# A chain of two mixings and two grouped convolutions on four row tiles: the first mixing moved from the whole array onto 32-row tiles

## The reference

```
# layers 0 and 2 ("mixing"): a matrix of its own for each sequence
h     = gelu(gelu(cond @ W0 + b0) @ W1 + b1)
att   = softmax(h @ W2 + b2)                    # 8 weights
agg_w = einsum('bk,koi->boi', att, weight)      # 128 x 128 for each sequence
x     = x + einsum('boi,bih->boh', agg_w, x) + (att @ bias_k)[:, :, None]
# layers 1 and 3 ("conv"): 4 groups of 32 channels, 9 taps, padding 4
x     = x + conv1d(x, w, groups=4) + (cond @ c_w.T)[:, :, None] + bias[:, None]
```

## Time and profile before

| | |
|---|---|
| median of 3 runs | 3080.31 us (3079.63 to 3084.73) |
| the profiled execution's own time | 3082.17 us |
| its span | 3080.3 us, mean granted clock 0.986 |
| PE / PEld busy | 97% / 86% |
| DVE / ACT / POOL busy | 44% / 44% / 58% |
| matmuls of the two convolutions (L301) | 36864 |
| matmuls of the second mixing (L316) | 6144 |
| matmuls of the first mixing (L289) | 1536 |
| DMA | 468.6 MB, the queue takes 47.7% of 16 engines |

### The profile page before, as it was taken

The page is one execution under the profiler, slowest core; times in us unless marked ns, Lnnn a source line. Parts: engine busy times, 40 slices in busy tenths (PEclk is TensorE's granted clock), DMA queues, the critical chain, the costliest instruction groups (busy, mean ns, idle before and its releaser), DMA issues.

```text
span 3080.3 us, 110157 instructions
## 1 busy us (share of the span) xinstructions
PE 3002.8 (97%) x44644; PEld 2650.9 (86%) x44644; DVE 1353.9 (44%) x2142; ACT 1362.7 (44%) x2358; POOL 1798.5 (58%) x1796
## 2 busy tenths in 40 slices
PE   4899999999999999999999999999999999999996
PEld 3788888888888888888888888888888888888885
DVE  5444444444444444444444444444444444444441
ACT  4344444444444444444444444444444444444442
POOL 0556656656655655655655655655655655655652
PEclk6999999999999999999999999999999999999998
DMA  7344444444444444444444444444444444444443
GB/s 317 103 146 153 152 145 154 152 145 154 152 145 154 152 145 154 152 145 154 152 145 154 152 145 154 152 145 154 152 145 154 152 144 154 152 144 155 152 145 105
DMA packets 229383, 468.62 MB, mean 152 GB/s; under 512 B 47336, under 2 KB 129392, under 8 KB 195312
## 3 DMA queue, kind: packets, MB, share of 16 engines
q1 hardware_dynamic: 229360, 468.30, 47.7%
HBM read 182.89 MB, written 150.99 MB: 108 GB/s over the span
## 4 chain that ended last, share of the span: by engine, by line
PE 96%; DMA 1%; DVE 1%; ACT 1%; SPq 0%; issue 0%; POOL 0%; POOLq 0%; DVEq 0%; ACTq 0%
PE ps L301 72%; PE ps L289 12%; PE ps L316 12%; DMA mixed<-work 1%; DMA conv_raw<-conv_w 0%; DVE y L571 0%; SPq L221 0%; DVE work L542 0%; ACT work L395 0%; PE ps L272 0%; DVE y L526 0%; DMA work<-mix_b 0%; ACT xp L382 0%; POOL work L628 0%; PE ps L244 0%
## 5 line engine op out<-in xcount | busy, mean ns | idle before, releaser
L301 PE MATMUL ps<-y,conv_parts 32*128 32x512 f32 x36864 | 2282.6, 392 | 6.8 <-DVE y L571 6.7
L301 PEld LDWEIGHTS ps<-y,conv_parts 32*128 32x128 f32 x36864 | 2026.2, 183 | 224.9 <-DVE y L571 81.0
L571 DVE SCALAR_TENSOR_TENSOR y<-ps,bias,y 128x512 fp32r<-128x512 f32 x1536 | 1035.6, 745 | 1662.4 <-ACT y L421 1662.3
L421 ACT ACTIVATE y<-ps,bias 128x512 fp32r<-128x512 f32 x1536 | 916.1, 699 | 721.1 <-PE ps L301 691.6
L609 POOL COPY bias<-bias_table 128x4 f32 (+1 forms) x512 | 324.5, 634 | 837.7 <-DMA work<-work 715.5
L621 POOL TENSOR_TENSOR xp<-x_t,xp 128x512 fp32r<-128x512 f32 x512 | 775.2, 1552 | 0.0
L448 ACT ACTIVATE work<-ps,bias 128x512 f32<-128x512 f32 x512 | 309.9, 689 | 853.9 <-PE ps L301 853.9
L628 POOL COPY work<-work 128x512 f32<-128x512 f32 x512 | 512.2, 1123 | 23.1 <-DMA work<-work 23.1
L613 POOL TENSOR_TENSOR m_parts<-m_raw,m_parts 128x128 fp32r<-128x128 f32 (+1 forms) x256 | 225.4, 880 | 416.6 <-ACT m_parts L428 416.6
L316 PE MATMUL ps<-y,m_parts 32*128 32x512 f32 x6144 | 414.0, 392 | 1.6 <-DVE y L571 1.5
L289 PE MATMUL ps<-xp,m_parts 128*128 128x512 f32 x1536 | 393.0, 404 | 20.7 <-POOL xp L621 20.7
(11 more groups left out here) (38 smaller groups left out, 36.4 us busy)
## 6 DMA issues: line engine op xcount, KB each, us to landing
x_t<-x SPq DMA_DIRECT2D x128, 1024.0 KB, 4.8
work<-work SPq DMA_DIRECT2D x2048, 64.0 KB, 2.0
out<-work SPq DMA_DIRECT2D x128, 1024.0 KB, 4.1
m_raw<-mixed SPq DMA_DIRECT2D x640, 64.0 KB, 3.3
mixed<-work SPq DMA_DIRECT2D x8, 2048.0 KB, 7.8
work<-mix_w SPq DMA_DIRECT2D x2, 2048.0 KB, 12.6
conv_raw<-conv_w SPq DMA_DIRECT2D x2, 768.0 KB, 10.9
work<-small SPq DMA_DIRECT2D x1, 852.0 KB
```

Source lines behind the costliest of these rows:

```text
L301: last = nc.tensor.matmul(ps[:, 4 + g, :], conv_parts[layer][rows, w, s, :], src[rows, a, p_in, q:q + N], start=(s == 0 and n == 0), stop= ...
L421: nc.scalar.activation(dst, ps[:, k if layer % 2 == 0 else 4 + k, :], ACT.Identity, bias=bias[layer][:, k:k + 1]).then_inc(high_set[layer], 1)
L571: nc.vector.scalar_tensor_tensor(out=dst, in0=ps[:, k if layer % 2 == 0 else 4 + k, :], scalar=bias[layer][:, k:k + 1], in1=high.bitcast(f ...
```

## The change

The first mixing is written like the second: 4 groups of 32 input channels, accumulated on four row tiles, where tile t now makes a quarter of *time* (512 consecutive points) rather than a phase, from x loaded so that partition 32q + c holds channel c of each group g at quarter q. It needs its matrix four times over (one copy for each 32 partitions), loaded and split like the second one's. Its banks hold quarters of time with all phases mixed, so ACT and DVE read a bank by phase (`by_phase`, every fourth element) and write four runs of 128 into `y1` (`segment`). PE's tasks are generated by one loop over rounds and tiles; with `LAG = 0` the order of the rounds is that of before, and in each round the four tiles follow each other. `x_high` waits once for the whole first mixing of the sequence before; the second mixing waits for `low` of layer 1 group by group.

```diff
-        x_t = sb("x_t", [128, T])
-        xp = sb("xp", [128, 2, PH, N], f32r)
+        x_t = sb("x_t", [128, G, N])
+        xp = sb("xp", [128, 2, G, N], f32r)
...
-        m_raw = {0: sb("m_raw0", [128, C]), 2: sb("m_raw2", [128, G, C])}
-        m_parts = {0: sb("m_parts0", [128, 2, C], f32r), 2: sb("m_parts2", [128, 2, G, C], f32r)}
+        m_raw = {l: sb(f"m_raw{l}", [128, G, C]) for l in (0, 2)}
+        m_parts = {l: sb(f"m_parts{l}", [128, 2, G, C], f32r) for l in (0, 2)}
...
+        def by_phase(q):
+            return ps[:, q, :].rearrange("c (m p) -> c p m", p=PH)
+        def segment(part, q):
+            return y1[:, part, :, 1 + q * (N // PH):1 + (q + 1) * (N // PH)]
...
-            def load_matrix0(j):
-                sp.dma_start(m_raw[0][:], scratch[0][bass.ds(j, 1)].rearrange("s (i o) -> (s i) o", i=C)).then_inc(m_in[0], 16)
-            def load_matrix2(j):
-                for p in range(PH):
-                    sp.dma_start(m_raw[2][CG * p:CG * (p + 1)],
-                                 scratch[1][bass.ds(j, 1)].rearrange("s (g c o) -> (s c) g o", g=G, c=CG)).then_inc(m_in[2], 16)
+            def load_matrix(layer, j):
+                for q in range(G):
+                    sp.dma_start(m_raw[layer][CG * q:CG * (q + 1)],
+                                 scratch[layer // 2][bass.ds(j, 1)].rearrange("s (g c o) -> (s c) g o", g=G, c=CG)).then_inc(m_in[layer], 16)
             def load_x(j):
-                sp.dma_start(x_t[:], x[j]).then_inc(x_in, 16)
+                for q in range(G):
+                    sp.dma_start(x_t[CG * q:CG * (q + 1)],
+                                 x[j].rearrange("(g c) (q n) -> q c g n", g=G, q=G)[q]).then_inc(x_in, 16)
...
-            def mix0(j, first):
-                pe.wait_ge(m_set[0], j + 1)
-                for p in range(PH):
-                    pe.wait_ge(x_low_set, nth(j, p))
-                    if not first:
-                        pe.wait_ge(low_set[2], nth(j - 2, p))
-                    for n, (m, a) in enumerate(PASSES):
-                        last = nc.tensor.matmul(ps[:, p, :], m_parts[0][:, m, :], xp[:, a, p, :], start=(n == 0), stop=(n == 2))
-                    last.then_inc(mm[0], 1)
+            MIX, CONV = G * len(PASSES), SHIFTS * len(PASSES)
+            ROUNDS = 2 * (MIX + CONV)
+            LAG = 0
+            def mix(layer, j, t, k, src, wait_src, wait_bank):
+                rows = slice(CG * t, CG * (t + 1))
+                g, n = divmod(k, len(PASSES))
+                m, a = PASSES[n]
+                if t == 0 and k == 0:
+                    pe.wait_ge(m_set[layer], j + 1)
+                if t == 0 and n == 0:
+                    pe.wait_ge(wait_src, nth(j, g))
+                if k == 0:
+                    wait_bank(t)
+                ins = nc.tensor.matmul(ps[:, t, :], m_parts[layer][rows, m, g, :], src[rows, a, g, :],
+                                       start=(k == 0), stop=(k == MIX - 1))
+                if k == MIX - 1:
+                    ins.then_inc(mm[layer], 1)
...
+            def step(i, inner):
+                for r in range(ROUNDS):
+                    for t in range(G):
+                        own = r - LAG * t
+                        if own >= 0:
+                            tile_round(i, inner, t, own)
+                        elif inner or i >= 0:
+                            tile_round(i - 1, inner, t, own + ROUNDS)
...
-                    for p in range(PH):
-                        high(0, i, p, y1[:, HIGH, p, 1:N + 1], not inner and i == 0)
+                    for q in range(G):
+                        high(0, i, q, segment(HIGH, q), by_phase(q), not inner and i == 0)
...
-                    for p in range(PH):
-                        low(0, i, p, y1[:, LOW, p, 1:N + 1], y1[:, HIGH, p, 1:N + 1])
+                    for q in range(G):
+                        low(0, i, q, segment(LOW, q), by_phase(q), segment(HIGH, q))
...
-                dve.wait_ge(x_in, 16 * (j + 1))
-                xv = x_t[:].rearrange("c (n p) -> c p n", p=PH)
-                for p in range(PH):
-                    if not first:
-                        dve.wait_ge(mm[0], nth(j - 1, p))
-                    nc.vector.tensor_copy(xp[:, HIGH, p, :], xv[:, p, :]).then_inc(x_high_set, 1)
+                dve.wait_ge(x_in, 16 * G * (j + 1))
+                if not first:
+                    dve.wait_ge(mm[0], 4 * j)
+                for g in range(G):
+                    nc.vector.tensor_copy(xp[:, HIGH, g, :], x_t[:, g, :]).then_inc(x_high_set, 1)
```

More of the change, by code:

```diff
@@ new lines, in conv @@
+            def conv(layer, j, t, k, src, wait_src, wait_bank):
+                rows = slice(CG * t, CG * (t + 1))
+                s, n = divmod(k, len(PASSES))
+                q, p_in = divmod(s, PH)
+                w, a = PASSES[n]
+                if k == 0:
+                    if t == 0:
+                        pe.wait_ge(wait_src, nth(j, PH - 1))
+                    wait_bank(t)
+                ins = nc.tensor.matmul(ps[:, 4 + t, :], conv_parts[layer][rows, w, s, :], src[rows, a, p_in, q:q + N],
+                                       start=(k == 0), stop=(k == CONV - 1))
+                if k == CONV - 1:
+                    ins.then_inc(mm[layer], 1)
@@ L322, in step, with tile_round, free0 @@
+            def tile_round(i, inner, t, r):
                 now, last, before = has(i, inner, 0), has(i, inner, 1), has(i, inner, 2)
-                if now:
-                    mix0(i, not inner and i < 2)
+                def free0(q):
+                    if inner or i >= 2:
+                        pe.wait_ge(low_set[2], nth(i - 2, q))
                 def free3(g):
@@ L342, in free1 @@
                         pe.wait_ge(low_set[1], nth(i - 1, g))
[L344 to L351, removed]
+                if r < MIX:
+                    if now:
+                        mix(0, i, t, r, xp, x_low_set, free0)
+                elif r < MIX + CONV:
+                    if before:
+                        conv(3, i - 2, t, r - MIX, y3, low_set[2], free3)
+                elif r < 2 * MIX + CONV:
+                    if last:
+                        mix(2, i - 1, t, r - MIX - CONV, y2, low_set[1], free2)
+                elif now:
+                    conv(1, i, t, r - 2 * MIX - CONV, y1, low_set[0], free1)
+            def step(i, inner):
[6 more added lines that the diff above has]
+                            tile_round(i - 1, inner, t, own + ROUNDS)
             steps(step)
@@ L412, in _, with high @@
             act.wait_ge(agg_mm, 2 * Q * QB)
-            def high(layer, j, k, dst, first):
+            def high(layer, j, k, dst, src, first):
                 act.wait_ge(mm[layer], nth(j, k))
@@ L451, in step @@
                     for p in range(PH):
-                        high(2, i - 1, p, y3[:, HIGH, p, 1:N + 1], not inner and i == 1)
+                        high(2, i - 1, p, y3[:, HIGH, p, 1:N + 1], ps[:, p, :], not inner and i == 1)
                 if now:
@@ L586, in step @@
                     for g in range(G):
-                        low(1, i - 1, g, y2[:, LOW, g, :], y2[:, HIGH, g, :])
+                        low(1, i - 1, g, y2[:, LOW, g, :], ps[:, 4 + g, :], y2[:, HIGH, g, :])
                 if now:
-                    for p in range(PH):
-                        low(0, i, p, y1[:, LOW, p, 1:N + 1], y1[:, HIGH, p, 1:N + 1])
+                    for q in range(G):
+                        low(0, i, q, segment(LOW, q), by_phase(q), segment(HIGH, q))
                 if has(i, inner, -1):
@@ L594, in step @@
                     for p in range(PH):
-                        low(2, i - 1, p, y3[:, LOW, p, 1:N + 1], y3[:, HIGH, p, 1:N + 1])
+                        low(2, i - 1, p, y3[:, LOW, p, 1:N + 1], ps[:, p, :], y3[:, HIGH, p, 1:N + 1])
             steps(step)
@@ L616, in x_low @@
             def x_low(j):
-                xv = x_t[:].rearrange("c (n p) -> c p n", p=PH)
-                for p in range(PH):
-                    pool.wait_ge(x_high_set, nth(j, p))
-                    nc.gpsimd.tensor_tensor(xp[:, LOW, p, :], xv[:, p, :], xp[:, HIGH, p, :].bitcast(fp32),
+                for g in range(G):
+                    pool.wait_ge(x_high_set, nth(j, g))
+                    nc.gpsimd.tensor_tensor(xp[:, LOW, g, :], x_t[:, g, :], xp[:, HIGH, g, :].bitcast(fp32),
                                             ALU.subtract).then_inc(x_low_set, 1)
```

20 lines of the change are left out of this document (9 added, 11 removed).

## The result

| | before | after |
|---|---|---|
| median of 17 runs | 3082.36 us (3078.75 to 3084.73) | 3087.14 us (3084.31 to 3089.18) |
| ratio | | 1.0015, 95% interval 1.0008 to 1.0022 |
| the profiled execution's own time, its span | 3082.17, 3080.3 | 3089.18, 3087.4 |

The change makes the kernel 4.8 us slower, +0.15%, which is within the 0.2% called "no change" above though the interval excludes zero. The forecast was +4 us and +0.13%. The 27 executions of the kernel before in one of the comparisons fall in two groups, 12 of 3078.9 to 3080.9 us at a mean granted clock of 0.987 or 0.988 and 13 of 3083.4 to 3084.9 us at 0.985 or 0.986, so a median of 3, as the 3080.31 of the prediction was, can stand 2 us beside that of 17.

The account below looks back on a forecast made before the run. Bound: the 3.50 us chain of ACT's and DVE's reads, not PE's work. Profiled execution 3082.2 + 4 (fill) + 0 x 127 = 3086.2; for the median, 3080.3 + 4 = 3084.3 us, +0.13%; range 3076 to 3096.

Parts of the forecast that it names:

- What bounds: Loop step: one ACT read, then DVE's four, set the fourth tile's start at 3.50 us; mix0 lies beside them.
- The switches, 0.25 us a step: Around mix0 on PE: 0.16 + 0.09 us a step removed, turning into a longer wait; taken as 0.
- the switches are paid for after all: Rival, in the loop: restart sooner by 0.25 us a step, gain 127 x 0.25 = 32, 3052 us; chance 0.11.
- Layer 0's reads by phase: ACT's and DVE's strided bank reads after the first mixing: 745 ns as now, costing only above 2.07 us each.
- POOL's contiguous x_low: POOL's low part of x on contiguous slices: 1.29 us for 1.50, four in the fill giving -0.8 us.
- x in the loop: Loads of x in the loop: landing 1.3 to 2.5 us later, with cover, so 0.
- The fill, +4: First sequence, before the loop, uncovered: terms sum to +3.8 us, taken as +4 (2 to 6).
- The tail: Fill, from the end of `x_low` to conv(1): 4.5 us instead of 2.59, so +1.9.
- The rhythm: Loop steps alternating 23.08 and 23.19 us might settle differently: -4 if all short, +10 if all long.
- the second rival: At conv(1)'s last round every step falls on ACT's late notice, 0.08 us each: 3094 us; chance 0.13.

Follow-up runs that it names:

- two cut kernels: Kernel before and changed kernel, each with ACT's and DVE's layer 1 work on 128 of 512 columns: 3052.64 us and 2987.65 us.
- run 1: Kernel before with ACT's and DVE's layer 1 work on 128 of 512 columns: 3052.64 us, ratio 0.9904.
- PE was kept busy: Changed kernel with useless matmuls into an unused bank while PE waits in the fill: 3085.90 us, ratio 1.0014.
- LAG = 1: Changed kernel with each tile one round behind the one before it, instead of none: 2995.77 us, ratio 0.9720.

## Why the prediction was right, and where it was not

- **What bounds.** Right, and for the reason given: the 3.50 us from ACT's first read to the fourth bank, seen with mix0 and without it, stood at 3.50 in the changed kernel and in the kernels with less and with more PE work (up to 3.51 with more). Cutting it short freed 99.5 us in the changed kernel.
- **The switches, 0.25 us a step.** This term was mis-sized: 0.58, from the two cut kernels. The working had 0.16 for the mixing's length, where the cut kernels show 0.19, and 0.09 for its entry, where they show 0.30; it had nothing for the 0.09 behind it. It didn't matter for the sum, since a gain beside the chain is worth nothing whatever its size; for the rival "the switches are paid for after all" it would have meant 3011 instead of 3052.
- **The chain's cost before.** Not a term of the sum, but the expectation of run 1 had it at 0.5 and it was 0.20: the first three tiles had run a round (0.235) in the 0.40 before the wait ended, and that round is not lost, since the fourth tile then stays a round behind.
- **Layer 0's reads by phase**: taken at 745 ns, measured 745. **POOL's contiguous x_low**: taken at 1.29 us, measured 1.296. **x in the loop**: expected late by 1.3 to 2.5 us; DVE now waits 1.3 us for it in a step, and nothing follows from it.
- **The fill, +4.** Its terms held up to the end of `x_low` (89.32 against 87.33, +2.0 for a worked-out +1.8). The tail was taken at +1.9 and was +2.8 (from there 5.43 us for 2.59), and the first conv(1) took 1.6 us more. Both are the clock, which the working left out altogether: the tail had the mixing's last three rounds at about 1.0, they took 1.9 at a clock of 0.50 (89.32 to 91.24) and 0.97 where PE was kept busy. The total was 6.7 in the profile, above the 6 given as its bound. Without the clock's 2.8 it is 3.9, the +3.8 of the working.
- **The agreement of the number.** In part it is luck. The medians differ by 4.8 and the two profiled executions by 7.0, and the working went by the profile. The forecast of 3084.3 also stood on the median of 3 executions, 3080.3; with the 3082.4 of 17 it would have been 3086.4, for the 3087.1 measured.
- **The rhythm.** Steps of 23.05 to 23.13 in the changed kernel with a mean of 23.104 against 23.109: neither end of the range was used, and the second rival did not occur. Its price was misread: 46.15 and 23.19 are distances between first matmuls of the mixing, which itself starts 0.06 or 0.12 us after ACT. ACT's own starts in the kernel before are 23.08 to 23.13 apart, and 74 of 124 steps were of the long kind already; if all were, it would cost 125 x 0.02, 2.5 us, not 10.

## What to carry to other kernels

A share of 96% in the chain that ended last says that an engine was busy, not that less work on it would help: look for a place where the same two events keep the same distance with and without that work. Where a task frees its banks one after another and the next one asks for all at once, the reads are exposed whatever the engine saves; setting the tiles apart by two rounds was worth 106 us here, once all tasks were on the same tiles. Moving the mixing to row tiles made that possible in this form, and its worth showed only with the second edit. What a lag would give the kernel before, with its whole-array mixing, no run shows.

## What the runs showed of the hardware

Eight matmuls fewer in a step made 65 of 125 steps slower by about 1.5 us (24.4 to 24.7 us, the other 60 took 23.1): with four matmuls in the 3.5 us of the chain, the granted clock fell to 1.2 GHz in the loop, with twelve it never did. DVE's cast of contiguous fp32 took 426 ns on average where one with a step of four elements took 626, while the same step cost nothing for DVE's and ACT's reads of a PSUM bank (744 and 688 ns in layer 0). A wait of the weight loads cost a row-tile stream less than it lasted: one of 0.29 us in a step (LAG = 1) made the step 0.10 longer than without waits, and waits of 0.30 and 0.48 one after the other (LAG = 0) made it 0.78 longer than with the chain cut short; there the other tiles' second round started only with the fourth tile, at 1513.86. Twelve whole-array matmuls between streams of row tiles took 0.58 us more than 48 on row tiles, half of it (0.30) ahead of their first matmul.
